# Two attention blocks and two expert blocks on one core: keys and values of the first attention projected during the threshold search

## The reference, cut to what matters

```python
x = x + _L0_xattn_ref(_layernorm(x), ctx_1024, ctx_1024, ...)      # no softmax over heads, exp of keys
x = x + _L0_ffn_ref(_layernorm(x), ...)                            # 8 experts, each takes its best 512 tokens
x = x + _L1_xattn_ref(_layernorm(x), ctx_1024, ctx_1024, mask, Wq, Wk, Wv, Wo)   # 16 heads of 16, softmax
x = x + _L1_ffn_ref(_layernorm(x), ...)                            # self attention, then top 2 of 8 experts
...
route_prob = jax.nn.softmax(xf @ Ws + bs, axis=-1).T               # of _L0_ffn_ref
route_vals, routes = jax.lax.top_k(route_prob, k)                  # k = 512 of 4096 tokens per expert
...
k = _heads(key @ Wk.T)                                             # of _L1_xattn_ref; key = value = ctx_1024
v = _heads(value @ Wv.T)
logits = jnp.einsum('bhqd,bhkd->bhqk', q, k) * SCALE
```

## Time and profile before

| | us |
|---|---|
| median of 3 runs | 2768.06 (2766.54 to 2769.54) |
| profiled execution, its own time | 2763.92 |
| its span | 2762.1 |
| threshold search, barrier to barrier (240.3 to 333.9) | 93.6 |
| first attention up to its first scores (632.5 to 699.6) | 67.1 |
| first attention from there to the last scores (699.6 to 1331.9) | 632.3 |

### The profile page before, as it was taken

The page is one execution under the profiler, slowest core; times in us unless marked ns, Lnnn a source line. Parts: engine busy times, 40 slices in busy tenths (PEclk is TensorE's granted clock), DMA queues, the critical chain, the costliest instruction groups (busy, mean ns, idle before and its releaser), DMA issues. The chain is left out here.

```text
span 2762.1 us, 39121 instructions
## 1 busy us (share of the span) xinstructions
PE 2310.8 (84%) x10904; PEld 1292.4 (47%) x10904; DVE 1339.5 (48%) x3501; ACT 1020.2 (37%) x1827; POOL 739.6 (27%) x764
## 2 busy tenths in 40 slices
PE   6694169994999999999589999999937999999991
PEld 2463146661343333443223333333316888888880
DVE  3555643313666666666257776777644111111115
ACT  2230012110455555556226555555611222232232
POOL 0110023334221022220142233332211333333335
PEclk9885579995999999999779999999967999999995
DMA  4310044426233244231043334323203666666654
GB/s 142 101 61 30 0 126 98 115 55 131 38 49 49 39 55 55 36 44 25 22 56 46 47 56 55 51 37 47 40 8 116 179 193 181 183 185 180 194 149 131
DMA packets 196359, 235.27 MB, mean 85 GB/s; under 512 B 21538, under 2 KB 177698, under 8 KB 195682
## 3 DMA queue, kind: packets, MB, share of 16 engines
q1 hardware_dynamic: 174498, 202.90, 32.0%
q0 software_dynamic: 21696, 30.42, 6.1%
HBM read 146.23 MB, written 35.91 MB: 66 GB/s over the span
## 5 line engine op out<-in xcount | busy, mean ns | idle before, releaser
L1728 DVE CUSTOM_DVE_ANT_0 atL1x_junk<-atL1x_pm,bias 128x512 bf16<-128x512 f32 x512 | 346.0, 688 | 228.7 <-PE atL1x_pm L1408 226.7
L1724 DVE TENSOR_REDUCE atL_tops<-atL_pm 128x1 f32<-128x512 f32 x512 | 339.7, 684 | 175.2 <-PE atL_pm L1408 169.3
L1565 ACT ACTIVATE atL1x_prob<-atL1x_ps 128x512 f32<-128x512 f32 x512 | 303.7, 598 | 288.5 <-PE atL1x_ps L1425 279.8
L1027 PE MATMUL exL_po<-exL_w,exL_hid 128*128 128x256 f32 x1760 | 393.2, 382 | 16.6 <-DVE exL_ys L1092 8.6
L1011 PE MATMUL exL_ph<-exL_xgT,exL_w 128*128 128x256 f32 (+1 forms) x1504 | 399.3, 421 | 6.0 <-ACT exL_hid L1043 3.6
L1565 ACT ACTIVATE atL_prob<-atL_ps 128x512 f32<-128x512 f32 x512 | 294.8, 599 | 254.3 <-PE atL_ps L1422 251.4
L1027 PEld LDWEIGHTS exL_po<-exL_w,exL_hid 128*128 128x128 f32 x1760 | 330.0, 190 | 71.1 <-issue 16.7
L1043 ACT ACTIVATE exL_hid<-exL_ph,exL_b 128x256 f32<-128x256 f32 (+1 forms) x376 | 190.1, 511 | 433.3 <-PE exL_ph L1011 412.2
L1011 PEld LDWEIGHTS exL_ph<-exL_xgT,exL_w 128*128 128x128 f32 x1504 | 276.8, 192 | 112.9 <-issue 59.6
L977 POOL DMA_INDIRECT sum<-exL_ys,exL_put x110 | 180.1, 1637 | 424.3 <-DVE exL_ys L1092 243.2
L1422 PE MATMUL atL_ps<-atL_qstack,atL_kstack 99*128 99x512 bf16 x512 | 201.5, 396 | 16.4 <-DMA atL_qstack<-atL_negT 5.8
(11 more groups left out here) (328 smaller groups left out, 2750.0 us busy)
## 6 DMA issues: line engine op xcount, KB each, us to landing
exL_w<-in_L_W SPq DMA_DIRECT2D x94, 1024.0 KB, 4.9
atL1x_kstack<-atL1x_k SPq DMA_DIRECT2D x96, 128.0 KB, 4.6
atL1x_qstack<-atL1x_q SPq DMA_DIRECT2D x96, 128.0 KB, 6.4
atL_kstack<-atL_k SPq DMA_DIRECT2D x96, 128.0 KB, 4.6
atL_qstack<-atL_q SPq DMA_DIRECT2D x96, 128.0 KB, 6.6
exL_b<-in_L_b SPq DMA_DIRECT2D x47, 128.0 KB, 5.4
sum<-tok_zero SPq DMA_DIRECT2D x1, 4224.0 KB, 15.5
aft_ctxT<-in_ctxT SPq DMA_DIRECT2D x2, 2048.0 KB, 10.1
```

Source lines behind the costliest of these rows:

```text
L1027: mm = pe.matmul(po[c % 2][:], hid[:, f, c * P:(c + 1) * P], w2[slot][:, f, :], start=f == 0, stop=f == FC - 1)
L1565: act.activation(prob[i % PROBS][:], ps[i % 2][:], ACT.Exp, scale=SCALE).then_inc(s["p_ready"], 1)
L1724: ins = dve.tensor_reduce(tops[g % 2][:, t, j:j + 1], pm[i % TOPS][:], AX.X, ALU.max)
L1728: ins = dve.tensor_tensor_reduce(junk[:, i % TOPS, :], pm[i % TOPS][:], G["bias"][0][:, t, :], 1.0, -BIG / 2, ALU.add, ALU.max, tops[g % 2 ...
```

## The change

In `expert_choice` the keys and values of the first attention are now computed for all 8 batches and stored in two DRAM tensors: `kstack`, the 96 stacked rows of key parts, and `values`, with the column of ones. SP loads `wk`, `wv` and the context per batch and issues the stores; PE projects (`keys`, `values`) behind each round's sum; ACT copies out of PSUM; POOL frames the values and cuts the keys. The rounds are written out instead of looped, and DVE shifts `pair` and `unit` right behind the count, in front of its wait for the sum; `unit` starts two bits higher. In the first attention the jobs k0, k1, v0, v1, the source load, POOL's key cuts and the key fills are gone; SP loads a batch's keys (two transfers) and values (one). POOL's first `clear` stands in front of the first norm and writes the ones of the key stack only. The second attention keeps its code.

```diff
@@ expert_choice, SP @@
+                sp.dma_start(wk[:], a["L1x_Wk"].rearrange("(c p) n -> p c n", p=P)).then_inc(wk_in, 16)
+                load_source(0)
+                sp.dma_start(wv[:], a["L1x_Wv"].rearrange("(c p) n -> p c n", p=P)).then_inc(wv_in, 16)
+                load_source(1)
+                for b in range(B):
+                    sp.wait_ge(k_cut, past((b + 1) * DC))
+                    for k, part in enumerate(K_TERMS):
+                        sp.dma_start(
+                            G["kstack"][b, :, k].rearrange("o d h s -> (d h) o s"), kparts[b % 2][part][:]
+                        ).then_inc(k_out[b % 2], 16)
+                    sp.wait_ge(v_saved, past((b + 1) * 2))
+                    sp.dma_start(G["values"][b], vals[b % 2][:]).then_inc(v_out[b % 2], 16)
+                    if b + 2 < B:
+                        sp.wait_ge(v_ps, past((b + 1) * 2))
+                        load_source(b + 2)
+                for i in range(2):
+                    sp.wait_ge(k_out[i], past(B // 2 * KOUT))
+                    sp.wait_ge(v_out[i], past(B // 2 * 16))
@@ expert_choice, ACT: copies of k (waits for k_cut two batches back) and v @@
...
@@ expert_choice, POOL @@
+                for b in range(B):
+                    for o in range(DC):
+                        x_, (hi, mid, lo) = kf[b % 2][:, o, :], (p[:, o, :] for p in kparts[b % 2])
+                        pool.wait_ge(k_saved, past(b * DC + o + 1))
+                        if b >= 2:
+                            pool.wait_ge(k_out[b % 2], past(b // 2 * KOUT))
+                        chain(pool.tensor_copy(hi, x_))
+                        chain(pool.tensor_tensor(x_, x_, hi, ALU.subtract))
+                        chain(pool.tensor_copy(mid, x_))
+                        pool.tensor_tensor(lo, x_, mid, ALU.subtract).then_inc(k_cut, 1)
@@ expert_choice, DVE @@
-                chain(dve.memset(unit[:], 1 << (BITS - 2)))
+                chain(dve.memset(unit[:], 1 << BITS))
...
-                with dve.Fori(0, ROUNDS) as i:
+                for i in range(ROUNDS):
...
                     dve.tensor_reduce(reach[:], cmp_[:], AX.X, ALU.add).then_inc(counted, 1)
+                    chain.mark(dve.tensor_scalar(pair[:], pair[:], 2, None, ALU.logical_shift_right))
+                    chain(dve.tensor_scalar(unit[:], unit[:], 2, None, ALU.logical_shift_right))
                     dve.wait_ge(totalled, past(i + 1))
...
-                    c(dve.tensor_scalar(pair[:], pair[:], 2, None, ALU.logical_shift_right))
-                    c(dve.tensor_scalar(unit[:], unit[:], 2, None, ALU.logical_shift_right))
@@ expert_choice, PE @@
-                with pe.Fori(0, ROUNDS) as i:
+                for i in range(ROUNDS):
                     pe.wait_ge(counted, past(i + 1))
                     pe.matmul(ptot[:, 0:STEPS * E], G["ones"][:], reach[:].rearrange("p k e -> p (k e)"),
                               start=True, stop=True).then_inc(totalled, 1)
+                    (values if i % 2 else keys)(i // 2)
...
                 in_front_pe(pe, G, pin, pall, more[:].rearrange("p e c -> p (e c)")).then_inc(totalled, 1)
+                values(B - 1)
@@ job_table @@
+    if not last and self_:
+        jobs += [(15, "a", "k0+"), (18, "a", "q0+"), (21, "a", "k1+"), (24, "a", "q1+"), (27, "a", "v0+"), (30, "a", "v1+")]
+    elif not last:
+        jobs += [(15, "a", "q0+"), (18, "a", "q1+")]
@@ attention, SP @@
-                    load_source(0)
                     if not self_:
+                        load_keys(0, 0)
+                        load_values(0, 0)
                         load_x(slice(CB, NC), "x_rest")
...
-                        sp.wait_ge(s["job_a"], past(J.base("a", b)))
+                        sp.wait_ge(s["s_ps"], past(b * PER))
                         alone(sp)
-                        load_source(b + 1)
+                        load_keys(b + 1, 1 - par)
                     negatives(b, par, 1, job_index("d", b, "neg1"))
+                    if not last and not self_:
+
+                        sp.wait_ge(s["pv_done"], past(b * NG * QUADS))
+                        alone(sp)
+                        load_values(b + 1, 1 - par)
@@ attention, POOL @@
                 def before():
+                    if not self_:
+                        clear(0)
                     norm(0)
-                    clear(0)
+                    if self_:
+                        clear(0)
                     cut(0, 0)
```

More of the change, by code:

```diff
@@ new lines, in _ @@
+            @block.gpsimd
+            def _(pool):
+                chain = Chain(pool, kchain)
+                for i in range(2):
+                    pool.memset(vals[i][:], 0.0).then_inc(framed, 1)
+                    pool.wait_ge(framed, past(2 * i + 1))
+                    pool.memset(value_heads(vals[i])[:, :, :, HD:HD + 1], 1.0).then_inc(framed, 1)
+                for b in range(B):
+                    for o in range(DC):
+                        x_, (hi, mid, lo) = kf[b % 2][:, o, :], (p[:, o, :] for p in kparts[b % 2])
+                        pool.wait_ge(k_saved, past(b * DC + o + 1))
+                        if b >= 2:
+                            pool.wait_ge(k_out[b % 2], past(b // 2 * KOUT))
[3 more added lines that the diff above has]
+                        pool.tensor_tensor(lo, x_, mid, ALU.subtract).then_inc(k_cut, 1)
@@ L576, in _ @@
                 assert chain.n == INIT
-                with dve.Fori(0, ROUNDS) as i:
[L578 to L583, removed]
+                shape = [P, STEPS, E]
@@ L596, in _ @@
-                chain = Chain(dve, vchain, ROUNDS * VPER + INIT)
+                        chain(dve.tensor_reduce(gained[:], took[:].rearrange("p k e -> p e k"), AX.X, ALU.add))
+                    chain(dve.tensor_tensor(low[:], low[:], gained[:], ALU.bitwise_or))
+                assert chain.n == ROUNDS * VPER + INIT
                 edge = wide(low[:].bitcast(F32))
@@ L1431, in value_quad @@
                     pe.wait_ge(s["p_ready"], past(b * PER + i + HG))
+                    if kc == 0 and g == 0 and not self_:
+                        pe.wait_ge(s["vals_in"], past((b + 1) * 16))
                     if kc == 0 and isinstance(b, int) and b == 0 and g == 0:
@@ L1515, in job @@
                         if not (isinstance(b, int) and b == 0):
-                            act.wait_ge(s[f"cut{i}"], past((b - 1) * 2 + (1 if kind == "k" else 2)))
+                            act.wait_ge(s[f"cut{i}"], past((b - 1) * len(cuts) + cuts.index(kind) + 1))
                         if self_:
@@ L1656, in before @@
                         keep(0, 0)
-                PPER = 12 + 1 + (3 if self_ else 0)
+                PPER = 6 * len(cuts) + 1 + (3 if self_ else 0)
                 def batch(b, par):
```

154 lines of the change are left out of this document (111 added, 43 removed).

## The result

The changed kernel takes 2722.11 us (median of 4 runs, 2718.44 to 2726.43) against 2767.32 (4 runs, 2766.54 to 2769.54): ratio 0.9836, 95% interval [0.9820, 0.9851], 45 us less. The forecast was 2728. Its profiled execution has a span of 2724.7 us, 37.4 less than before.

| stretch (us) | before | after | difference | forecast |
|---|---|---|---|---|
| search: rounds, first candidates to `more` | 79.34 | 88.01 | +8.7 | +17 |
| search: `more` to the next stage's first DVE instruction | 12.84 | 19.14 | +6.3 | +5 |
| attention: load of x to the first transpose | 16.55 | 9.08 | -7.5 | -7.2 |
| attention: first transpose to first maxima | 27.30 | 20.57 | -6.7 | -6.7 |
| attention: first to last scores | 632.3 | 586.4 | -45.9 | -49 |

The account below looks back on a forecast made before the run. PE was taken to bound the attention's steady part, DVE and its round trip to PE the search. Search +22, start -13, batches -49 gave -40: 2728 us, own range 2714 to 2742, wider range 2702 to 2752.

Parts of the forecast that it names:

- The batches: First attention, seven batches: k and v projections leave PE, 7.0 us a batch, -49 us; bounds 40 and 59.6.
- Rival D: First attention: batches keep their length because of late keys or DVE; total +9, 2777 us; chance 0.03.
- The attention's start: First attention's start: early clearing saves 7.2 us, q0 first shortens 27.3 to 20.6; taken as -13, bounds 7 and 16.
- DVE's round: Search: shifts beside the count and a smaller loop gap cut a round from 5.30 to 4.4 us, -13.5 in 15 rounds.
- The collision: Search: POOL's cuts hold DVE 1.9 us a round, rounds of 6.3 us, +26.6 in 14 rounds; bounds 0 and 49.
- PE's round: Search: PE's block takes 3.5 us at full clock, about 7.3 at low; cold first and later blocks cost +4 us.
- the transfers: Search: 22 MB, 62 us at 353 GB/s, hidden beside about 95 us of rounds; SP's issues 5 us of 12.6.
- the prediction's signs: Search 110 to 120 us, DVE's comparison and OR in two lengths, first maxima after some 32 us, batches of 74 us.
- The end: Search's end: last key block, cut and stores take 19 us from the last count against 14.4; +5, bounds 0 and 12.
- A: Search: no collision, POOL and DVE share freely, search level within a few us; about 2702 us; chance 0.17.
- B: Search: PE stays cold, rounds take 120 us and the search about 137; 2749 us; chance 0.18.
- C: Search: transfers bound it, 22 MB taking 195 us if stores run like fills; +39, 2807 us; chance 0.05.

Follow-up runs that it names:

- experiment 5: The changed kernel with PE's k0, k1, v0, v1 work put back into each first-attention batch as repeated q projections, results overwritten: 2777.30 us, ratio 1.0042.
- experiment 4: The kernel before, with POOL's clearing, values' memsets included, in front of the first attention's norm: 2758.23 us, ratio 0.9969.
- experiment 3: The kernel before, with only the search's rounds written out and the two shifts put beside the count: 2756.47 us, ratio 0.9956.
- experiment 2: As experiment 1, but POOL's key cuts are left out and the first attention works with constant key parts: 2695.55 us, ratio 0.9740.
- experiment 1: The changed kernel with SP loading the source of batch b+2 in front of batch b's key and value stores: 2707.42 us, ratio 0.9776.
- Experiment 7: As experiment 6, with the last value block between the two rank sums and its values stored before the last key stores: 2703.08 us, ratio 0.9762.
- experiment 6: As experiment 1, with SP's semaphore clearing behind its first search loads and POOL's clearing before the second attention's norm: 2699.01 us, ratio 0.9752.
- experiment 8: As Experiment 7, with ACT instead of POOL writing the keys' first bf16 part straight from PSUM: 2700.06 us, ratio 0.9760.

## Why the prediction was right, and where its steps were off

**The batches (-49 forecast, -45.9 measured).** Right in mechanism, and by experiment 5 for the reason given: 16 + 8 records at their spacing. A batch gave back 45.8 / 7 = 6.5 us instead of 7.0. Put back alone they cost 6.9; the 0.4 us a batch between the two are 2.4 us in seven, no more than traces of the same batches differ by (3.4 us), so nothing is shown to take them away. Rival D is settled with it: no new wait for keys or DVE, PE at 97%.

**The attention's start (-13, measured -14.2).** Both halves came at their size: 7.5 us for the clearing (7.2 forecast; experiment 4, the move alone, shows 6.65, because the values' two memsets were moved with it and the norm's root then waited for them), and 6.7 us for q0 in front (20.57 us from the transposes to the maxima, where 20.6 had been worked out).

**DVE's round.** Forecast 5.30 to 4.4, -13.5 us. Measured without neighbours 4.15, -17.1 (experiment 3). The step that was off: I took the 0.11 us between two chained instructions for a property of the chain. It is the loop's, as the ranks behind it show already before the change; written out, five such gaps a round shrink to 0.03 or 0.04. With PE warm it is 3.95 (experiment 2), a second gain that no step had.

**The collision.** Forecast 6.3 us a round, 1.9 us of it collision, +26.6; measured 4.81 and 0.86, 11 us in thirteen rounds. The mechanism is the one of the earlier trace rows: the OR ends with the subtraction in front of it. The size fell for the step "since POOL's next is ready before DVE's next (0.08 against 0.11 us), nearly in full". The two numbers were the wrong way round here: DVE's next instruction comes 0.03 us behind the last, POOL's 0.07 or 0.08, so DVE's comparison is there ahead of POOL's second subtraction, and it is POOL that waits, for 1.05 us. The rows show this order; no run changed the gaps alone. In a round DVE is held 0.63 us at the OR and 0.23 at the comparison; their sum is the 0.86. The Trainium skill (SBUF — State Buffer, § Who interferes with whom) says "Issue order, not op shape, decides who blocks": the runs agree, with the comparison at 1.55 us beside a POOL subtraction of 2.50 in one lock and at 2.31 beside one of 1.20 in another. The prediction read from the section's rule that the term lies between 26.6 and 49 us, and it measured 11: the rule alone does not give the size, since that hangs on the order.

**PE's round and the transfers.** "The first key block is cold ... +4 us, together with a later cold block or two": the first one cost 3.2 (round 7.42 against the 4.17 ahead of it). The later cold blocks were three, and they were not the clock's doing: PE waited 4.4 or 4.5 us each time for a source that SP had queued behind stores. "Hidden beside about 95 us of rounds" was right for bytes (204 GB/s of the 348 that experiment 2 reached) and "5 us of 12.6" was right for SP's issues (3.48 + 0.72 + 0.68 us a batch), but neither asks what the load stands behind: the stores wait for POOL's cut, and with them the source. That cost 14.0 us (88.0 - 74.0, experiment 1) and stands in no term.

**Where luck came in.** The rounds came out at +8.7 instead of +17. Against the forecast the collision was 15.4 us smaller (26.6 - 11.2), and the sources behind the stores, which no term had, cost 14.0: two mistakes that nearly cancelled. What is left is DVE's round (3.6 us more gained), the warm count (0.2 us a round in thirteen rounds) and the cold blocks (3.2 instead of 4). That the total lies within 6 us of the forecast is owed to this luck. One of the prediction's signs missed: the search takes 108 us, where 110 to 120 was to show the collision.

**The end (+5, measured +6.3).** The price was about right, its reason not: the last to land is the value store, which waits for PE's last block behind both rank sums; the key stores that I had timed were issued 2.2 us before (until 345.70). Experiment 7 takes 2.5 of the 6.3 back.

**The rivals.** A (no collision) falls by the two lengths of OR and comparison; experiment 2, that kernel made real, is 12 us below experiment 1. B (PE cold throughout) falls: the clock is 0.83 in the stage, and 1.00 in experiment 1 with PE 82% busy. (The clock at the attention's start before rose 16.0 us behind the first transposes, at 666.7, and not the 13 of the text.) C falls with 204 and 348 GB/s, though SP's order of stores and loads did hold three rounds up. D falls with the batches.

## What to carry to other kernels

Work moved from a stage whose bound it is (PE at 97%) into one where its engine idles is worth its spacing at full clock, instruction by instruction; price the stage that takes it up by three questions: which instructions of the critical engine can be held by a neighbour's and who gets there first, what each load stands behind in its queue, and which block is the last to land. A load that frees a wait on PE goes in front of stores that wait for a slow engine: here that order alone was worth 14 us, nearly as much as the rounds' whole rewriting (17) and more than the collision (11). And move large memsets to where their neighbours wait for data: 6.6 to 7.5 us each time, in both attentions.

## What the runs showed of the hardware that was not expected

- Two engines that meet every round lock in a pattern, and the pattern sets the price: rounds of 4.81 and 4.93 us for the same instructions, 4.37 with two casts less in two rounds. In experiments 6 and 7, with the first source there 1.1 us earlier, it was the second pattern and not the first, but no run shows that this was the cause: experiment 5 has the code of the change in its search, had another start (rounds of 4.17, 9.93, 5.04, 4.17, 4.93, 6.91, 5.00 us, with comparisons of 2.31 in the fifth) and settled at 4.81.
- The one that comes second is held for a little less than the two overlap. The OR overlaps with the subtraction for 0.78 us and takes 0.63 longer, the comparison with the cast for 0.44 and takes 0.23 longer; in experiment 6 the comparison overlaps for 0.99 and takes 0.79 longer. The difference is 0.13 to 0.20 us each time.
- A shift of 3 uint32 per partition waits for POOL's subtraction like a large instruction (0.77 us instead of 0.16), while reductions never changed (0.95 us in every kernel).
- PE, 82% busy with gaps of 0.9 us, kept 2.4 GHz for 71.7 us in experiment 1, where 140 to 226 us of the kernel before had a mean of 0.82 with PE 92% busy. A wait of 4.4 or 4.5 us stood beside each of the three falls to 1.2 GHz for 6.8 us; in experiments 5 and 8 waits of 1.6 and 2.0 us stood just ahead of a fall for 3.4 us.
- Stores from 128 partitions and the source loads ran together at 348 GB/s (experiment 2), where fills into 16 partitions had 113, with the DMA engines full in both.
